# Attention over 2048 keys on one Trainium2 core: keys' parts stored once per chunk, a start on batch 0 alone, and the later squarings moved

## The reference, cut to what matters

```python
q = (layernorm(x) @ Wq.T + bq).reshape(B, 128, 16, 8)      # 16 heads of 8
k = (ctx @ Wk.T + bk);  v = (ctx @ Wv.T + bv)              # 2048 keys, same heads
attn = softmax(q @ k.T / sqrt(8) + mask, over the keys)    # mask is zeros in the data
x = x + (attn @ v) @ Wo.T + bo
sigma_in, sigma_out = largest singular values of W_in, W_out
x = x + gated linear recurrence over the tokens of layernorm(x), W_in and W_out divided by max(sigma, 1)
x = x + MLP(layernorm(x)) with weights mean(|w|) * sign(w), gelu, 512 hidden
```

## Time and profile before

| what | us |
|---|---|
| median of 3 runs | 326.34 (326.28 to 327.01) |
| the profiled execution | 329.18 |
| its span, first to last instruction | 327.4 |
| PE busy in the span | 257.0 (79%) |
| DVE busy | 231.3 (71%) |
| ACT busy | 200.7 (61%) |
| POOL busy | 108.2 (33%) |

### The profile page before, as it was taken

One profiled execution on the slowest core, in us unless ns is written; L12 is line 12 of the kernel. 1 busy time (PEld: TensorE's weight loads), 2 busy tenths in 40 slices (PEclk: granted clock), 3 DMA queues, 4 the chain that ended last, 5 costly groups with the idle time before them and its releaser, 6 DMA issues.

```text
span 327.4 us, 9590 instructions
## 1 busy us (share of the span) xinstructions
PE 257.0 (79%) x3904; PEld 160.6 (49%) x3904; DVE 231.3 (71%) x425; ACT 200.7 (61%) x309; POOL 108.2 (33%) x267
## 2 busy tenths in 40 slices
PE   0799615499999999999999999999999877550276
PEld 0577401245555556555565655555655444440156
...
GB/s 146 381 88 220 226 179 292 363 153 50 148 92 153 146 50 161 107 127 145 52 188 102 103 50 77 73 50 50 80 68 52 3 4 2 0 0 0 0 0 32
DMA packets 24565, 34.48 MB, mean 105 GB/s; under 512 B 2444, under 2 KB 19112, under 8 KB 24392
## 3 DMA queue, kind: packets, MB, share of 16 engines
...
q0 software_dynamic: 128, 0.14, 0.5%
q10 hardware_dynamic: 676, 0.33, 0.3%
...
## 4 chain that ended last, share of the span: by engine, by line
PE 58%; ACT 17%; SPq 6%; DMA 6%; DVE 6%; issue 5%; POOL 2%; POOLq 0%; ACTq 0%; DVEq 0%
PE ps L447 15%; ACT probs L739 13%; PE ps L434 13%; PE ps L418 6%; PE ps L320 4%; PE ps L357 4%; SPq L259 4%; PE ps L487 3%; PE ps L495 3%; DMA k_rows_dram<-k_parts 2%; DMA w_kv<-in_L_xattn_Wq_dram 2%; PE ps L455 2%; PE ps L667 2%; PE ps L340 2%; DMA ctx_buf<-in_ctx_dram 1%
## 5 line engine op out<-in xcount | busy, mean ns | idle before, releaser
L1191 DVE TENSOR_REDUCE pmax<-ps 128x2 f32<-128x1024 f32 x128 | 156.1, 1224 | 42.8 <-PE ps L418 41.0
L739 ACT ACTIVATE probs<-ps 128x1024 f32<-128x1024 f32 x128 | 130.8, 1022 | 47.2 <-PE ps L434 47.2
L447 PE MATMUL ps<-probs,v_now 128*9 128x128 f32 x2048 | 82.4, 280 | 0.2 <-ACT probs L739 0.2
L434 PE MATMUL ps<-q_max,k_rows 51*128 51x128 bf16 x1024 | 52.3, 223 | 13.9 <-ACT probs L739 12.8
L447 PEld LDWEIGHTS ps<-probs,v_now 128*9 128x9 f32 x2048 | 43.8, 91 | 34.9 <-issue 33.1
L418 PE MATMUL ps<-k_rows,q_now 48*128 48x512 bf16 x256 | 51.2, 398 | 11.0 <-DMA k_rows<-k_rows_dram 8.3
L968 POOL CAST max_cols<-negmax 128x2 bf16<-128x2 f32 x32 | 6.1, 192 | 133.6 <-DVE negmax L1197 133.6
L434 PEld LDWEIGHTS ps<-q_max,k_rows 51*128 51x128 bf16 x1024 | 30.0, 96 | 37.5 <-ACT probs L739 22.7
L418 PEld LDWEIGHTS ps<-k_rows,q_now 48*128 48x128 bf16 x256 | 12.8, 96 | 14.2 <-DMA k_rows<-k_rows_dram 8.5
L690 ACT ACTIVATE ctxT<-ps 128x512 f32<-128x512 f32 x16 | 9.6, 597 | 14.2 <-PE ps L320 14.2
L357 PE MATMUL ps<-power 128*128 128x128 f32 x96 | 16.7, 297 | 0.2 <-DVE power L1119 0.2
...
## 6 DMA issues: line engine op xcount, KB each, us to landing
...
```

Source lines behind the costliest of these rows:

```text
L434: t = pe.matmul(dst, k_rows[rows, i % 4, at:at + P], q_max[rows, i % 2, :], start=not masked, stop=True, skip_group_check=masked)
L447: t = pe.matmul(ps[at:at + HEAD_COLS, 6, 0:P], v_now[:, i % 2, 4 * c + j, HEAD_COLS * h:HEAD_COLS * h + HEAD_COLS], probs[:, c, h, P * j:P ...
L739: act.activation(probs[:, u % CHUNKS, :, :], ps[:, 4:6, :], ACT.Exp).then_inc(probs_ready, 1)
L1191: dve.tensor_reduce(pmax[:, i % 2, :, c], ps[:, bank:bank + 2, :], AX.X, ALU.max).then_inc(pmax_ready, 1)
```

## The change

1. Memory holds each key part once: `store_k` is one DMA of 384 KB a chunk. A contraction now has 56 rows a head: three key parts against query part 1, the same three against part 2, and key part 1 against part 3. `load_half_pair` loads a head with two DMAs: 48 rows (24 rows of memory read twice, 192 KB) and 8 rows (32 KB). So a pair is four DMAs, 448 KB.
2. Start: only chunks 0 to 3 are prepared before the first scores, with the queries of batch 0 alone. Pair 0 is loaded chunk by chunk; the second heads of pairs 0 (upper half of the keys) to 3 are loaded from POOL's queue. Chunks 4 to 7 and the other queries are done by PE and ACT between scores 0 to 7, and their keys are cut by POOL, all four steps of chunk 4+i in pair i's turn, for i from 0 to 3. The buffer of ctx chunks has 6 slots in place of 8.
3. SP's list is written anew: ctx chunk 8 comes after the stores of chunks 4 and 5, and the load of pair 4 after the stores of chunks 6 and 7. Chunks 8 to 15 are cut by POOL in pairs 4 to 19 (before: 2 to 17).
4. The Gram products and their norm move to units 55 and 63, all 24 squarings to units 64 to 111, four every eight units (at places 0, 2, 3, 4 of the eight), and the turned weights to place 6. The means and signs of the MLP's weights move into DVE's units 42 and 44.
5. `v_now` and `q_now`, POOL's copies of a pair's values and queries, are gone; the products read `v_all` and `q_all`. The sum of |mask| is made by ACT.

```diff
 HEAD_COLS = 9
 SQUARINGS = 24
...
     FIRST = 2 * CHUNKS
+    CTX_SLOTS = 6
     LEAD = 8
-    EARLY_SQUARES = 6
     SQUARE_UNITS = 64
...
+        def store_k(eng, n):
+            b, c = divmod(n, CHUNKS)
+            eng.dma_start(k_dram[b, :, :, 512 * c:512 * c + 512], k_parts[:, :, 512 * n:512 * n + 512]
+                          ).then_inc(k_stored[b % 2] if b else k_first[c], 16)
+
+        def load_half_pair(eng, i, h, keys, loaded):
+            b, p = divmod(i, PAIRS)
+            at, first = HALF_ROWS * h, 16 * p + HD * h
+            n = keys.stop - keys.start
+            triples = k_dram[b, first:first + HD, :, keys].rearrange("r i n -> (r i) n")
+            eng.dma_start(k_rows[at:at + 2 * TRIPLE, i % 4, keys],
+                          triples.rearrange("(a m) n -> a m n", a=1).broadcast_to((2, TRIPLE, n))).then_inc(loaded, 16)
+            eng.dma_start(k_rows[at + 2 * TRIPLE:at + ROWS, i % 4, keys], k_dram[b, first:first + HD, 0, keys]
+                          ).then_inc(loaded, 16)
...
+            def load_pair(i):
+                wait(sp, keyscores_ready, CHUNKS * (i - 3))
+                for h in range(2):
+                    load_half_pair(sp, i, h, all_keys, k_rows_loaded[i % 4])
+
+            def store_chunk(n):
+                sp.wait_ge(k3_ready, n + 1)
+                store_k(sp, n)
...
+            store_q_parts(first_tokens, 0, 1)
+            store_chunk(0)
+            sp.wait_ge(once("q_stored"), 16 * 3)
+            sp.wait_ge(once("q_all_zeroed"), 1)
+            load_q(sp, first_tokens, once("q_loaded"))
+            sp.wait_ge(once("k_ones_ready"), 1)
+            store_chunk(1)
+            for c in range(2):
+                sp.wait_ge(k_first[c], 16)
+                for h in range(2):
+                    load_half_pair(sp, 0, h, slice(512 * c, 512 * c + 512), k_first[c])
+                load_ctx(CTX_SLOTS + c)
+                store_chunk(2 + c)
+            for c in (2, 3):
+                sp.wait_ge(k_first[c], 16)
+                load_half_pair(sp, 0, 0, slice(512 * c, 512 * c + 512), k_first[c])
+            for i in range(1, 4):
+                load_half_pair(sp, i, 0, all_keys, k_rows_loaded[i])
+            for n in range(EARLY, EARLY + 2):
+                store_chunk(n)
+            store_q_parts(rest_tokens, 4, 2)
+            load_ctx(FIRST)
+            load_ctx(FIRST + 1)
+            sp.dma_start(w1_nat[:, :, :], w1.rearrange("(a p) d -> p a d", p=P)).then_inc(ld["mlp"], 16)
+            sp.dma_start(w2_nat[:, :], w2).then_inc(ld["mlp"], 16)
...
+            sp.wait_ge(once("q_stored"), 16 * 6)
+            load_q(sp, rest_tokens, once("q_loaded"))
...
+            for n in range(FIRST + 2, FIRST + 4):
                 load_ctx(n)
...
-            def store_k(n):
-                b, c = divmod(n, CHUNKS)
-                sp.wait_ge(k3_ready, n + 1)
-                keys = slice(512 * c, 512 * c + 512)
-                for first, parts in K_GROUPS:
-                    sp.dma_start(k_dram[b, :, first:first + parts, keys],
-                                 k_parts[:, 0:parts, 512 * n:512 * n + 512]
-                                 ).then_inc(k_stored_rest if b else k_stored_first, 16)
...
-            def load_pair(i):
-                b, p = divmod(i, PAIRS)
-                wait(sp, keyscores_ready, CHUNKS * (i - 3))
-                for h in range(2):
-                    sp.dma_start(k_rows[HALF_ROWS * h:HALF_ROWS * h + ROWS, i % 4, :],
-                                 k_dram[b, 16 * p + HD * h:16 * p + HD * h + HD, :, :].rearrange("r i n -> (r i) n")
-                                 ).then_inc(k_rows_loaded[i % 4], 16)
...
-            store_k(3)
-            sp.wait_ge(once("k_ones_ready"), 1)
-            sp.wait_ge(k_stored_first, 16 * len(K_GROUPS) * CHUNKS)
-            for i in range(4):
-                load_pair(i)
-            for n in range(CHUNKS, FIRST):
-                store_k(n)
-            small_vectors()
-            for n in range(FIRST, ALL_CHUNKS):
-                load_ctx(n)
+            for n in range(EARLY + 2, FIRST):
+                store_chunk(n)
             for i in range(4, ALL_PAIRS):
...
-                    sp.wait_ge(k_stored_rest, 16 * len(K_GROUPS) * CHUNKS * (i // PAIRS))
+                    sp.wait_ge(k_stored[i // PAIRS % 2], 16 * CHUNKS * (2 if i // PAIRS == 3 else 1))
                 load_pair(i)
+                if i % 2 == 1 and FIRST + 4 + (i - 5) // 2 < ALL_CHUNKS:
+                    load_ctx(FIRST + 4 + (i - 5) // 2)
                 if i >= 6 and i % 2 == 0 and FIRST + i // 2 - 3 < ALL_CHUNKS:
-                    store_k(FIRST + i // 2 - 3)
+                    store_chunk(FIRST + i // 2 - 3)
...
+            def turn_xn(bank, first, n):
+                for i in range(first, first + n):
+                    t = turn(ps[:, bank, P * i:P * i + P], xn[:, i, :])
+                t.then_inc(once("xn_turned"), 1)
+
+
+            turn_ctx(0, 0)
+            pe.wait_ge(ld["wk"], 16)
+            turn(ps[:, 2, 0:P], w_kv[:, 0, :])
+            pe.wait_ge(ld["vec_qk"], 32)
+            pe.transpose(ps[:, 2, 3 * P:3 * P + 2], vec_nat[0:2, :], ident[0:2, 0:2]).then_inc(once("kqv_turned"), 1)
+            turn_ctx(1, 1)
+            pe.wait_ge(once("kT_ready"), 1)
+            project_k(4, 0)
+            pe.wait_ge(ld["wq"], 16)
+            turn(ps[:, 2, P:2 * P], w_kv[:, 2, :]).then_inc(once("kqv_turned"), 1)
+            pe.wait_ge(once("xn_ready"), 1)
+            turn_xn(3, 0, 1)
+            turn_ctx(0, 2)
+            project_k(5, 1)
...
+                if i == 0:
+                    pe.wait_ge(k_first[c], 16 + (LOADS if c < 2 else LOADS // 2))
+                    if c == 0:
+                        pe.wait_ge(once("q_loaded"), 16 * 2)
+                    elif c == 2:
+                        pe.wait_ge(second_heads[0], LOADS // 2)
+                elif c == 0:
+                    if i < 4:
+                        pe.wait_ge(second_heads[min(i, 2)], LOADS // 2 if i == 1 else LOADS)
+                    pe.wait_ge(k_rows_loaded[i % 4], LOADS * (i // 4) + (LOADS // 2 if i % 4 else 0))
+                    if i == PAIRS:
+                        pe.wait_ge(once("q_loaded"), 16 * 4)
...
+                elif n == ALL_CHUNKS - 2:
+                    pe.wait_ge(v_half_ready, 2 * m + 2)
+                    pe.wait_ge(ld["ssm"], 32)
+                    for w in range(2):
+                        t = pe.matmul(ps[:, 7, P * w:P * w + P], w_nat[:, w, :], w_nat[:, w, :], start=True, stop=True)
+                    t.then_inc(sq_done, 1)
+                elif n == ALL_CHUNKS - 1:
+                    pe.wait_ge(v_half_ready, 2 * m + 2)
+                    sum_norms(0)
 
...
+                k = SQ_PERIOD * m
                 if at == 0:
-                    if m == 0:
...
-                        pe.wait_ge(fro_inv_ready, 2 * (k // SQ_PERIOD) + 1)
-                    square(7, k)
+                    pe.wait_ge(fro_inv_ready, 2 * m + 1)
+                    square(k)
...
                 elif at == 2:
                     side_taken(i)
-                    square(7, k + 1)
...
+                elif at == 3:
+                    square(k + 2)
+                elif at == 4:
+                    square(k + 3)
...
             def attend(masked):
-                for u in range(6):
-                    scores(u, masked)
+                scores(0, masked)
+                early_k(4)
+                early_turn(5)
+                early_v(4)
+                scores(1, masked)
+                early_k(5)
+                early_turn(6)
+                pe.wait_ge(v_ready, 3)
+                pe.wait_ge(once("xn_ready"), B)
+                turn_xn(6, 1, B - 1)
+                early_v(5)
+                scores(2, masked)
+                early_k(6)
+                early_turn(7)
+                pe.wait_ge(once("qT_ready"), 4)
+                pe.matmul(ps[:, 6, T:TOK], kvT[:, 2, :], xnT[:, T:TOK], start=True, stop=True
+                          ).then_inc(once("q_done"), 1)
+                early_v(6)
+                scores(3, masked)
+                early_k(7)
+                scores(4, masked)
+                early_v(7)
+                scores(5, masked)
                 pe.wait_ge(once("out_bank_zeroed"), 1)
                 turn_max(0).then_inc(turned, 1)
-                for u in range(6, LEAD):
-                    scores(u, masked)
+                pe.wait_ge(ctxT_ready, FIRST)
+                pe.wait_ge(k32_ready, FIRST - EARLY)
+                scores(6, masked)
                 keyscores(0, masked)
+                scores(7, masked)
+                pe.wait_ge(v_ready, FIRST)
                 for g in range(UNITS):
...
             def side_squares(g):
                 m, at = divmod(g - SQUARE_UNITS, 8)
-                k = EARLY_SQUARES + SQ_PERIOD * m
...
+            gp.memset(max_cols[:, :, :], 0.0).then_inc(once("pads_ready"), 1)
             gp.wait_ge(once("ones_ready"), 2)
```

(39 more changed lines are left out.)

608 lines of the change are left out of this document (289 added, 319 removed).

## The result

The changed kernel takes **442.8 us** (median of 4 runs, 441.4 to 444.2) against 326.7 for the kernel before: 1.355 times as long, 95% interval 1.349 to 1.360. I had said 341 with a range to 425. The time lies beside the "two engines" rival (420), not beside my sum.

A forecast was written before the change was run, and what follows sets the result against it. PE and ACT together were taken to set the pace, after a start-up of PE waits. Terms -8.0, +9.8, +2.8, +7.2, +2.7 gave +14.5 on the profiled 329.18 (343.7), less 2.84 to the median: 341 us, range 329 to 425.

The forecast's parts named there:

- two engines: Rival, large k_rows loads: two engines carry each, a pair takes 8.2 us; +94, 420 us in all; chance 0.28.
- my sum: Whole kernel: five terms totalling +14.5 us, with k_rows loads landing in 2.6 to 3.7 us; 341 us.
- lands 3.3 later: Pair 4 and odd pairs 7 to 21: the second large k_rows load lands 3.3 us after its issue.
- Start-up, -8.0: Start up to unit 2's exponential: it comes at 57.7 instead of 65.70 us, -8.0, bounds -12 and -4.
- Pair 4, +9.8 and +2.8 for the clock: Scores of unit 16: PE waits 9.8 us for pair 4's load behind chunk 7's store; the fallen clock adds 2.8.
- Pairs 7 to 21, +7.2: Odd pairs' loads behind new chunk stores: a stop of 0.9 us every eight units, eight times, +7.2; bounds 1.6 to 38.
- Squarings, +2.7: Four squarings instead of three per eight units, plus turned weights, Gram products, means and signs: +2.7 us (1 to 4).
- Slower: Whole kernel: the change makes it slower; chance 0.83, from forecast 0.45, two engines 0.28 and crowded queues 0.10.
- faster: Rival, start-up: unit 2's exponential at 49, before 52, gaining 16.7 us; -3 in all, 323 us; chance 0.12.

The follow-up runs named there:

- e5: Changed kernel with the two copies inside the 24 rows in the 48-row load's source, not outermost, queries' rows reordered to match: 382.1 us.
- e8: e5 with SP issuing ctx chunks 8 and 9 ahead of the stores of chunks 4 and 5 and of the queries' rest: 363.4 us.
- e9: e5 with each new chunk in the loop stored behind the load of the next odd pair, not ahead of it: 339.5 us.
- e13: e5 with ctx 8, 9 and pair 4 loaded before stores, later chunks stored behind odd loads, weights and queries' rest loaded later, signs in four places: 309.7 us.

## Why the prediction was wrong, point by point

**The step that failed** is "lands 3.3 later" for the large load, and with it the choice between sum and rival. Every load of `k_rows` in the trace had 48 outermost on both sides; I gave a load with 2 outermost the price of the nearest row, and the two-engine case, whose price I had worked out at 420, a chance of 0.28. The row was for another shape: in the changed kernel the pair's loads land 9.8 after the last is out, and swapping the two dimensions alone takes 60.7 us off (e5). The measured time is 22.8 above that rival: it had pair 4 at 17.6 behind unit 8 (measured 19.45), eight units in 21.7 (measured 23.7 from unit 22 to 30), and 8.2 a pair behind the last store (48.88 us for six pairs, 8.15).

The 3.3 was also too low for a good shape. I wrote that all loads of `k_rows` land in 2.6 to 3.7, but the earlier trace rows has them only from 66 to 130 us. The eight loads of the kernel before that were given out together at 43.5 to 47.1, of the same shape, took:

```profile
DMA to landing us min/median/max: 3.1/5.2/7.2
```

That row was in the same trace, and it is near the 4.7 of e5's pair 9.

**Start-up, -8.0.** Measured -3.35 in the changed kernel, a smaller gain than my bound of -4, and -5.5 in e5. The chain was the right one (POOL's cut of chunk 5, the stores, ctx 8), but it began later: pair 1's negated maximum came at 49.02 where I had 45 (in e5 46.11), and from there to unit 2's exponential it took 13.3 where I had 12.6 (in e5 14.1). Unit 0's exponential was at 43.54, past my 39 to 43, and in e5 at 41.16. The second heads are eight issues on POOL and not the 12 that I counted. What I did not see is how cheaply the wait could be undone (e8).

**Pair 4, +9.8 and +2.8 for the clock.** In e5, without the shape's cost, PE stands 11.0 us and goes on 12.5 behind unit 8's exponential, where I had 9.8 and 11.3; the clock is at 0.50 in the stop and up to 88 us. From unit 8 to unit 16 it is 26.12 us against 13.41, +12.7, and my two terms make +12.6. So they were right together, with the wait 1.2 too small and the clock too dear by about as much; that they meet so well is partly luck. In the changed kernel the same stretch takes 35.36, +22.0.

**Pairs 7 to 21, +7.2.** The term that was most wrong apart from the shape: the eight stops cost 45.5 in e5, past my bound of 38 too, and e9 gets 42.6 back. The moment at which POOL is done was right to 0.15 us. Two things were missing: the queues are not half empty behind a store, since four issues, ctx and the next pair's load follow at once (+2.0: 0.5 until the second large load is issued, 1.4 on its landing); and a stop lets the clock fall, which I had counted once, at pair 4, and not here. My rows held it: the earlier trace rows showed the fall after PE ran dry. The waits themselves, 2.1 to 3.0 where I read them, are about half of the 45.5.

**Squarings, +2.7.** In e13, where nothing covers it, units 64 to 112 take 80.63 against 79.14 before, +1.5, and units 11 to 64 +0.7, 0.5 of it at the signs: 2.2 in all, right in size. But the signs of the weights, which I put at 0.3, cost 3.0 in e9 (4.74 against 1.75 before unit 40) when they stood in one block, and nothing in the changed kernel, where a stop covers them.

**Direction.** "Slower" (0.83) was right, and so were the waits that I named. The "faster" rival failed at its own point, unit 2 before 52; with the order put right that point is passed (47.54). Its sum holds a slip besides: 9.1 and 1.6 make 10.7 and not 12.7, so its 323 should have been 321.
